# Mamba's prologue on one Trainium2 core: where the weights are split, which table the first silu uses, and which engine sums the first block's softplus

## The reference

```python
x = x + 0.5 * _L0_ffn_ref(_layernorm(x), ...)
x = x + _L0_attn_ref(_layernorm(x), ...)      # Mamba forward plus Mamba on the flipped sequence
...
def _mamba_dir(h, ...):
    xz = h @ in_proj_w.T
    x, z = (xz[..., :D_INNER], xz[..., D_INNER:])              # D_INNER = 256
    x = jax.nn.silu(_causal_depthwise_conv(x, conv_w, conv_b))  # 4 taps
    x_dbl = x @ x_proj_w.T
    dt = jax.nn.softplus(x_dbl[..., :DT_RANK] @ dt_proj_w.T + dt_proj_b)
    Bm = x_dbl[..., DT_RANK:DT_RANK + D_STATE]                 # D_STATE = 16
    Cm = x_dbl[..., DT_RANK + D_STATE:]
    A = -jnp.exp(A_log)
    y = _selective_scan(x, dt, Bm, Cm, A, D)                   # h = exp(dt*A)*h + dt*x*B; y = h.C + D*x
    y = y * jax.nn.silu(z)
    return y @ out_proj_w.T
```

## Time and profile before

| what | value |
|---|---|
| three timed runs | 3114.83, 3117.87, 3124.79 us |
| median | 3117.87 us |
| profiled execution, span from first to last instruction | 3183.4 us |
| profiled execution, mean granted TensorE clock | 0.913 |
| busy share of that span: PE, DVE, ACT, POOL | 83%, 74%, 55%, 45% |
| Mamba phase in the trace | about 335 to 1425 us |

### The profile page before, as it was taken

The page is one execution under the profiler, slowest core; times in us unless marked ns, Lnnn a source line. Parts: engine busy times, 40 slices in busy tenths (PEclk is TensorE's granted clock), DMA queues, the critical chain, the costliest instruction groups (busy, mean ns, idle before and its releaser), DMA issues. The chain is left out here.

```text
span 3183.4 us, 38531 instructions
## 1 busy us (share of the span) xinstructions
PE 2649.1 (83%) x11128; PEld 1684.0 (53%) x11128; DVE 2342.8 (74%) x4109; ACT 1746.4 (55%) x3003; POOL 1430.6 (45%) x1514
## 2 busy tenths in 40 slices
PE   6888378889889989867888589949888889885999
PEld 5666233333334334225766467736555556553877
DVE  6688279989999999987688544477878777764444
ACT  3467365546556646523566345536776667763554
POOL 2465578888878878863464440031211111110000
PEclk9899688989899989996899789969999999996999
DMA  2146222222222222211146200000000000001000
GB/s 66 34 131 133 76 62 64 70 64 72 64 70 72 72 67 70 73 57 54 36 134 115 66 26 1 0 12 1 1 1 2 2 1 1 1 1 37 7 7 13
DMA packets 99373, 146.10 MB, mean 46 GB/s; under 512 B 12892, under 2 KB 50524, under 8 KB 98980
## 3 DMA queue, kind: packets, MB, share of 16 engines
q1 hardware_dynamic: 82052, 98.41, 10.5%
q0 software_dynamic: 16608, 44.78, 6.4%
q10 hardware_dynamic: 512, 0.53, 0.1%
HBM read 124.78 MB, written 18.87 MB: 45 GB/s over the span
## 5 line engine op out<-in xcount | busy, mean ns | idle before, releaser
L1634 POOL TENSOR_TENSOR a_hc<-a_H,a_cb 128x512 f32<-128x512 f32 x512 | 622.4, 1226 | 191.0 <-DVE a_H L1527 160.5
L1339 PE MATMUL a_Y<-a_hc,ident 128*128 128x512 f32 x1024 | 533.1, 640 | 36.8 <-POOL a_hc L1634 34.8
L2074 DVE TENSOR_REDUCE a_mx<-a_W 128x1 f32<-128x512 f32 (+3 forms) x768 | 397.2, 550 | 159.0 <-PE a_W L1878 104.7
L1980 ACT ACTIVATE a_pt<-a_W 128x512 f32<-128x512 f32 (+3 forms) x768 | 353.2, 492 | 227.8 <-PE a_W L1891 224.9
L1446 ACT ACTIVATE a_dA<-a_dt,a_aneg 128x512 f32<-128x512 f32 x512 | 339.7, 714 | 207.9 <-DVE a_H L1527 114.8
L1339 PEld LDWEIGHTS a_Y<-a_hc,ident 128*128 128x128 f32 x1024 | 182.7, 196 | 264.7 <-POOL a_hc L1634 134.8
L1891 PE MATMUL a_W<-a_Q,a_K 128*128 128x512 f32 (+3 forms) x768 | 303.2, 400 | 4.4 <-issue 2.3
L2222 POOL TENSOR_TENSOR a_spare<-a_zero 128x1 f32<-128x1 f32 x128 | 27.1, 212 | 582.7 <-ACT a_pt L1980 582.7
L1875 PE MATMUL a_W<-a_K,a_Q 128*128 128x512 f32 (+3 forms) x768 | 274.9, 365 | 10.8 <-DVE a_mx L2074 10.5
L411 ACT ACTIVATE m_raw<-m_U,m_wg 128x512 f32<-128x512 f32 x248 | 173.6, 701 | 127.7 <-PE m_U L306 122.9
L1009 DVE TENSOR_TENSOR t_hl<-t_raw,t_hh 128x512 fp32r<-128x512 f32 x128 | 88.1, 691 | 209.3 <-ACT t_hh L924 184.6
(11 more groups left out here) (311 smaller groups left out, 6432.0 us busy)
## 6 DMA issues: line engine op xcount, KB each, us to landing
a_cb<-a_crow SPq DMA_DIRECT2D x256, 256.0 KB, 3.2
m_orows<-m_yt SPq DMA_DIRECT2D x46, 256.0 KB
t_wst<-ternary_w SPq DMA_DIRECT2D x22, 256.0 KB, 2.9
m_xrows<-m_pool SPq DMA_DIRECT2D x16, 256.0 KB, 2.3
m_xg<-m_xrows,m_gidx POOLq DMA_INDIRECT x184
out<-x SPq DMA_DIRECT2D x8, 256.0 KB, 2.3
m_wg<-moe_ws SPq DMA_DIRECT2D x2, 516.0 KB, 4.4
a_hc<-mamba_conv_rows SPq DMA_DIRECT2D x1, 1024.0 KB
```

The lines of the kernel that those rows point to most:

```text
L1339: pe.matmul(Y[:, h, :], ident[:], hc[:, g % HCRING, :], start=False, stop=v == NS - 1).then_inc(s_y, 1)
L1634: pool.tensor_tensor(hc[:, G % HCRING, :], H[:, s, span], cb[:, v % RING, :], ALU.mult).then_inc(s_hc, 1)
L1980: act.activation(pt[:, u % PR, 0:BLK - r * P], W[:, 3 + u % 3, 0:BLK - r * P], ACT.Exp).then_inc(s_exp, 1)
L2074: dve.tensor_reduce(dst, W[:, s % 3, 0:min(BLK, (t + 1) * P - c * BLK)], AX, ALU.max)\
```

## The change

Five edits, all in `mamba`, all for the prologue:

1. VectorE: the products of the conv rows and the low parts `wzl` and `wcl` stand in front of `returned(0)`, the first statistics and `normalize(0)`.
2. GpSimd: the memset of `H` stands behind the first eight fetches, and the constants that others wait for are four, not five.
3. ScalarE: the phase begins with the silu table. For block 0's chunk (`tb == 0`) `o_read` applies silu with its bias directly from PSUM into `xs`; behind the second half it waits for its own result, loads the table set with exp and ln, and makes aneg there. The silus of block -1 are gone. TensorE's first x projection waits for s_Oa, and the later ones for one s_xs less.
4. VectorE, not GpSimd, makes the two sums, dt and u of block 0 (`b < 0`), each with the same lag; within a step in the order rl, um, dt, u. They stand ahead of the block of step 3 in the text of the loop.
5. VectorE: the copy of `sel` stands in front of the wait for s_aexp and the product with -1.

```diff
--- before.py
+++ after.py
@@ -1138,7 +1138,7 @@
     def silus_of(b):
 
         if b == -1:
-            return {4: (0, None)}
+            return {}
         if b == 0:
             return {4: (1, None), 12: (2, 0)}
         t = b % 4
@@ -1300,7 +1300,10 @@
                         pe.matmul(O[:], wzl[:, f], xh[:, padded(c)], start=False, stop=False)
                         mm = pe.matmul(O[:], wzh[:, f], xl[:, padded(c)], start=False, stop=True)
                     elif kind == "xp":
-                        pe.wait_ge(s_xs, tb + 1)
+                        if tb == 0:
+                            pe.wait_ge(s_Oa, through("A", b, v - 1))
+                        else:
+                            pe.wait_ge(s_xs, tb)
                         for h in range(HALF):
                             mm = pe.matmul(O[0:DBL, :], xpw[:, e, h, :], xs[:, tb % 4, h, :],
                                            start=h == 0, stop=h == 1)
@@ -1363,8 +1366,8 @@
 
             @block.scalar
             def _(act):
-                nc.scalar.preload_act_table_set("natural_log_exp_and_others")
-                act.wait_ge(s_cst, 5)
+                nc.scalar.preload_act_table_set("silu_and_others")
+                act.wait_ge(s_cst, 4)
                 act.activation(xh[:, 0:PADW], pads[:], ACT.Copy).then_inc(s_pad, 1)
                 act.activation(xl[:, 0:PADW], pads[:], ACT.Copy).then_inc(s_pad, 1)
                 act.activation(xh[:, PADW + SEQ:], pads[:], ACT.Copy).then_inc(s_pad, 1)
@@ -1374,7 +1377,6 @@
                 act.wait_ge(s_wc, 1)
                 act.activation(wcv[0], taps, ACT.Copy).then_inc(s_wh, 1)
                 act.wait_ge(s_ld, 16 * len(LOADS))
-                act.activation(aneg[:], alog[:], ACT.Exp).then_inc(s_aexp, 1)
 
                 def o_read(b, v, use):
                     kind, part, tb = use
@@ -1384,6 +1386,13 @@
                     act.wait_ge(s_O, through("O", b, v))
                     if kind == "T":
                         act.activation(xh[:, padded(c)], O[:], ACT.Copy).then_inc(s_xh, 1)
+                    elif kind == "x" and tb == 0:
+                        act.activation(xs[:, 0, part, :], O[:], ACT.Silu, bias=vecs[:, 0, 0, part:part + 1])\
+                           .then_inc(s_Oa, 1)
+                        if part == 1:
+                            act.wait_ge(s_Oa, through("A", b, v))
+                            nc.scalar.preload_act_table_set("natural_log_exp_and_others")
+                            act.activation(aneg[:], alog[:], ACT.Exp).then_inc(s_aexp, 1)
                     elif kind == "x":
                         act.activation(xs[:, tb % 4, part, :], O[:], ACT.Copy).then_inc(s_Oa, 1)
                     elif kind == "z":
@@ -1526,16 +1535,16 @@
                         out, a, bb = out[:, ::-1], a[:, ::-1], bb[:, ::-1]
                     dve.tensor_tensor_scan(out, a, bb, init, ALU.mult, ALU.add).then_inc(s_scan, 1)
 
-                returned(0)
-                statistics(GROUPS[0])
                 dve.wait_ge(s_ldw, 32)
                 for k in range(2 * TAPS):
                     last = dve.tensor_tensor(taps[:, k, :], taps[:, k, :], wi[:, 0:256], ALU.mult)
                 last.then_inc(s_wc, 1)
-                normalize(0)
                 dve.wait_ge(s_wh, 2)
                 dve.tensor_tensor(wzl[:], wi[:, 256:512], wzh[:].bitcast(F32), ALU.subtract).then_inc(s_wl, 1)
                 dve.tensor_tensor(wcv[1], taps, wcv[0].bitcast(F32), ALU.subtract).then_inc(s_wl, 1)
+                returned(0)
+                statistics(GROUPS[0])
+                normalize(0)
 
                 for b in range(-1, NB + 1):
                     uses = uses_of(b)
@@ -1574,6 +1583,26 @@
                             dve.wait_ge(s_O, through("O", b, v - 2))
                             xb = x[:, i * SEQ + c * BLK:i * SEQ + (c + 1) * BLK]
                             dve.tensor_tensor(xb, xb, O[:], ALU.add).then_inc(s_Od, 1)
+                        if b < 0:
+                            if slot_of(b, 3, "dt")(v):
+                                _, part, _ = uses[v - 3]
+                                dve.wait_ge(s_ln, part + 1)
+                                dve.tensor_tensor(rl[:, part, :], rl[:, part, :], ln[:], ALU.add).then_inc(s_sr, 1)
+                            if slot_of(b, 4, "dt")(v):
+                                _, part, _ = uses[v - 4]
+                                dve.wait_ge(s_um, part + 1)
+                                dve.tensor_tensor(um[:, part, :], um[:, part, :], ee[:], ALU.subtract).then_inc(s_co, 1)
+                            if slot_of(b, 5, "dt")(v):
+                                _, part, _ = uses[v - 5]
+                                dve.wait_ge(s_sr, part + 1)
+                                dve.wait_ge(s_co, part + 1)
+                                dve.tensor_tensor(dt[:, 0, part, :], rl[:, part, :], um[:, part, :],
+                                                  ALU.subtract).then_inc(s_dt, 1)
+                            if slot_of(b, 6, "dt")(v):
+                                _, part, _ = uses[v - 6]
+                                dve.wait_ge(s_dt, part + 1)
+                                dve.tensor_tensor(u[:, 0, part, :], dt[:, 0, part, :], xs[:, 0, part, :],
+                                                  ALU.mult).then_inc(s_u, 1)
                         if (b, v) == (-1, 3):
                             returned(1)
                             statistics(GROUPS[1])
@@ -1583,10 +1612,10 @@
                                     last = dve.tensor_scalar(diag[:, e, h, :], ident[:], vecs[:, 2, e, h:h + 1], None,
                                                              ALU.mult)
                             last.then_inc(s_pre, 1)
+                            dve.wait_ge(s_sel, 16)
+                            dve.tensor_copy(sel[:], sels).then_inc(s_pre, 1)
                             dve.wait_ge(s_aexp, 1)
                             dve.tensor_scalar(aneg[:], aneg[:], -1.0, None, ALU.mult).then_inc(s_pre, 1)
-                            dve.wait_ge(s_sel, 16)
-                            dve.tensor_copy(sel[:], sels).then_inc(s_pre, 1)
                             normalize(1)
 
             @block.gpsimd
@@ -1595,8 +1624,7 @@
                 pool.memset(one[:], 1.0).then_inc(s_cst, 1)
                 pool.memset(mone[:], -1.0).then_inc(s_cst, 1)
                 pool.memset(pads[:], 0.0).then_inc(s_cst, 1)
-                pool.memset(H[:], 0.0).then_inc(s_cst, 1)
-                pool.wait_ge(s_cst, 5)
+                pool.wait_ge(s_cst, 4)
 
                 def root(n):
                     t = GROUPS[n]
@@ -1613,6 +1641,7 @@
                     fetched[0] += count
 
                 fetch(2 * TPB)
+                pool.memset(H[:], 0.0).then_inc(s_cst, 1)
                 root(0)
                 fetch(2 * TPB + 4)
                 root(1)
@@ -1639,6 +1668,8 @@
                             lo = slice(0, 2 * NS)
                             pool.tensor_tensor(bcs[lo, tb % 4, :], dbl[lo, tb % 2, :],
                                                bcs[lo, tb % 4, :].bitcast(F32), ALU.subtract).then_inc(s_bcs, 1)
+                        if b < 0:
+                            continue
                         if slot_of(b, 6, "dt")(v):
                             _, part, tb = uses[v - 6]
                             pool.wait_ge(s_dt, 2 * tb + part + 1)
```

## The result

| | before | after |
|---|---|---|
| timed runs, median (lowest to highest) | 3119.8 us (3114.8 to 3126.7), 8 runs | 3102.5 us (3097.5 to 3113.0), 8 runs |
| ratio | | 0.9944, 95% interval 0.9928 to 0.9959 |
| P: from GpSimd's first memset of the phase to VectorE's first product of block 0 | 63.60 us | 46.85 us |

The changed kernel is 17.3 us, 0.56%, faster; the interval leaves 13 to 22 us. The forecast was 3102.4. That it was met to 0.1 us is luck: the gain forecast was 15.5 us, taken off a median of 3117.9, and the kernel before took 3119.8 beside the change.

A forecast was written before the change was run, and what follows sets the result against it. The prologue was taken as one chain up to VectorE's first product at 399.23 us, with the loop following. Gains 3.3 + 2.5 + 1.7 + 2.1 + 5.9 = 15.5 us off 3117.9 gave 3102.4, range 3096 to 3111.

The forecast's parts named there:

- Step 1: Prologue's front: weights split under the fetch, H's memset behind eight fetches, so xl and the conv products start 3.3 us earlier.
- It just gets through: GpSimd's eighth fetch, issued 344.8 to 345.8, clears wcl at 346.1; a slip of 0.4 us would lose 2.4 us.
- Step 2: Before the x projection: silu straight from PSUM replaces copy, table load and two silus on the chain; gain 2.5 us.
- Step 3: x projection: a shorter idle gap on TensorE keeps full clock, 1.94 us instead of 3.66; gain 1.7 us.
- I count nothing: The dt projection behind the x projection could give 0.9 us at full rate; left out of the sum.
- Step 4: First half's sum and um on VectorE end the second exp's 2.09 us wait for GpSimd; gain 2.1 us.
- step 5: Tail from second ln to first product: six VectorE instructions, 4.25 us instead of 10.1 on GpSimd; gain 5.9 us.
- A: Part of the front lost: fetch caught under wcl (2.4 us), projection at half rate (1.7), or ScalarE idle (1.0); chance 0.22.
- B: The block loop gives the gain back through 6 us more waits on GpSimd's u and TensorE; 3108.5, chance 0.11.
- C: VectorE becomes late for the first half's rl sum, beyond 2.7 us of slack; 3108 and up, chance 0.04.
- D: Slower: loop waits on TensorE grow by over 25 us, at half rate in more blocks; 3127.2 and more, chance 0.03.
- E: Something other than u holds the first product, so the tail's gain shrinks; 3108 at worst, chance 0.03.

The follow-up runs named there:

- a_repeat: The changed kernel, unchanged, profiled again on another chip: P 49.34 us, ratio 0.9969 to the kernel before.
- e6_order: Changed kernel with VectorE's dt and u of half 0 ahead of half 1's rl sum, and wzl earlier: P 48.41 us, ratio 0.9953 to the kernel before.
- e4_memset: Changed kernel with H's memset back ahead of the fetches, ScalarE waiting for five constants again: P 50.80 us, no ratio.
- e5_gap: Changed kernel with two spare table loads (2.57 us) ahead of the second silu: P 51.93 us, no ratio.
- e6_repeat: The kernel of e6_order, unchanged, profiled again: P 47.81 us, no ratio.
- e8_nofetch: Kernel before, sums left on GpSimd, the eight fetches between them moved into block 0: P 58.92 us, one time 3187.6 us beside a median of 3186.2.
- e9_early: Changed kernel with the diagonal matrices and the copy of sel ahead of the second eight merges and their statistics: P 47.25 us, no ratio.
- e7_best: Changed kernel with e9_early's move and e6_order's order of sums, without its early wzl: P 45.87 us, ratio 0.9942 to the kernel before.
- e1_front: Kernel before with only the weights' split ahead of the first merge and H's memset behind eight fetches: P 59.69 us, ratio 0.9981.

## Why the prediction was right, point by point

- **What bounds it.** That the prologue is one chain is shown: the parts of the change, step by step below, add up to P's 16.75 us. That the loop keeps what it is given is shown as well: the distance from the first product of block 0 to that of block 15 is 960.2 and 960.3 us in the two profiles before and 959.1 and 957.4 in those of the changed kernel, and the whole Mamba phase is 17.6 us shorter. That it all arrives in the time is shown on the first chip. On that of a_repeat it is not: P, 49.34, is 14.3 us less than before, but the ratio leaves 6 to 14 us, less than the 15.5 forecast. In the other five kernels with a ratio the gain in P lies inside the interval.
- **Step 1, front, 3.3 us forecast, 3.5 measured.** The merge started right behind wcl. "It just gets through" held, with more room than I gave it: what is held is a fetch that starts inside wcl. The eighth started 0.95 us ahead of wcl, and in e6_order one that started 0.51 us ahead was not held, though VectorE then idled 0.57 us. So the slip of 0.4 us, which I priced at 2.4, would have cost about 0.6 at most (an estimate from e6_order). e4_memset, with a slip of 1.6, shows the price of a held one: 2.5 us. So it is the moved memset of H that keeps the fetch out of wcl, as reckoned. The Trainium skill (SBUF — State Buffer, Who interferes with whom) has it that two SBUF inputs on VectorE contend with a GpSimd instruction that reads SBUF, and the 2.48 us fetch agrees with that; that a tensor_tensor was not seen to stall a DMA, for which it infers a reason, does not hold for these indirect fetches.
- **Step 2, silu, 2.5 us forecast, 2.4 measured.** A silu of 128x512 from PSUM took 0.69, as taken, and the product followed 0.25 us behind it, not 0.14. The drain that the Trainium skill (ScalarE: Activation LUTs, What ACT_TABLE_LOAD costs) adds was not there: aneg's exp started 0.01 us behind the load of 1.28 us.
- **Step 3, clock, 1.7 us forecast, 1.75 measured.** e5_gap shows that the gap does it: 0.98 us of idle and full clock, 3.55 and half.
- **The one term mis-sized: the dt projection**, "I count nothing". My reason was the idle of over 1 us in between; it was 1.21 us and cost no clock. The product was at full clock and gave 0.95 us, which is most of what P fell short of the forecast (46.85 against 48.1). It had stood in the range. It is also the least certain: in e6_order, a_repeat and e6_repeat, behind 2.77, 2.65 and 2.59 us of idle, it took 2.04, 1.97 and 1.70 us.
- **Step 4, 2.1 us forecast, 2.2 measured; step 5, 5.9 forecast, 6.0 measured.** Six instructions in 4.11 us, with the 2.34 us of idle ahead of the second rl sum that the program order leaves. e8_nofetch parts what I had taken together: over half is the queue of fetches.
- **Rivals.** A's caught fetch occurred in neither profile of the changed kernel, and in e4_memset when provoked. Its projection at half rate did not occur, but in a_repeat a late dbl and a dt projection that lost the clock cost 2.3 us, which I had not thought of. ScalarE did not idle behind its table load. B: the loop's length from block 0 to block 15 lay between 957.2 and 960.3 us in all runs but e8_nofetch (964.2, with the eight fetches more); it gave nothing back. C: VectorE waited 2.0 us for the first ln, slack 2.7 forecast. D and E did not occur.

Not settled: why the changed kernel's ratio was 0.9944 on one chip and 0.9969 on another. P accounts for 2.5 us of the 8 between them; the intervals just touch.

## What to carry to other kernels

Before a transfer's wait comes work that needs only what has landed; but look at what the other queues do beside it, since a long two-input VectorE instruction holds up a fetch that starts on GpSimd meanwhile (2.5 us here). Elementwise sums at the end of a chain cost what stands between them in the queue as much as what they take: count the fetches. And a gap shortened ahead of a matmul pays twice, once as time and once as clock, though the second part comes and goes.

## What the runs showed of the hardware

- An indirect fetch that started while VectorE ran its 2.29 us subtraction of two SBUF tensors took 2.48 us instead of 0.94 (e4_memset), as the one of 2.28 us in the earlier trace rows. One that had started 0.51 us ahead of it took 0.94 (e6_order). Beside the eight short products of 0.35 us fetches took at most 1.09.
- GpSimd's power on 128x4 elements took 2.15 us beside VectorE's 1.21 us copy of sel (after) and 1.05 away from it (e9_early, e7_best).
- ScalarE's read of four matmuls began 1.1 to 1.6 us behind their modelled end at a granted clock of 1.00 in four profiles, each time within 0.07 us of the end of a 1.21 us copy on VectorE; in the others it began 0.04 us behind.
- TensorE kept the full clock across 0.98, 1.21 and 2.27 us of idle (after; the last in e4_memset, where the dt projection took 1.10 us) and had lost it after 3.42 and 3.55 us, once to regain it inside the next 3.27 us (e1_front).
- The same program has a span of 3183.4 us in one profile and 3116.6 in another, and medians of 3123.8, 3186.2 and 3184.3 us on three chips, while the prologue of Mamba is 63.60 and 63.62 us in the two profiles.
